# The pooled stage moved into the block of the later layers, with its products by feature rows and the first dense unit beside its last batch

## What is computed

```
x = layernorm(x + pooled(x));  x = layernorm(x + dense(x))
x = layernorm(x + heads(x));   x = layernorm(x + experts(x))

pooled: h  = layernorm(x) * g + b
        q, k, v = h Wq + bq, h Wk + bk, h Wv + bv
        w  = exp((q Wqa + bqa) / sqrt(512));  w = w / cumsum(w)
        mixed = cumsum(w * q) * k
        u  = exp((mixed Wka + bka) / sqrt(512));  u = u / cumsum(u)
        result = cumsum(u * mixed) * v
dense:  (silu(x Wg) * (x Wu)) Wd, weights dequantised from integers, 2048 inner features
```

## Time and profile before

| what | value |
|---|---|
| median of three runs | 3158.72 us |
| the profiled execution | 3159.45 us, its span 3157.6 us |
| busy in the span: PE, DVE, ACT, POOL | 2993.2, 1829.1, 1172.4, 1091.7 us |
| mean granted clock of TensorE | 0.973 |
| start of the dense products | 391.56 us |

### The profile page before, as it was taken

How to read it: one execution, slowest core, us unless ns; L and a number is a source line. 1 busy time by engine, 2 the same in 40 slices (tenths; PEclk the granted TensorE clock), 3 DMA queues, 4 the chain that set the end, 5 groups by cost and what they waited for, 6 DMA issues and landing times.

```text
span 3157.6 us, 38080 instructions
## 1 busy us (share of the span) xinstructions
PE 2993.2 (95%) x13984; PEld 2482.2 (79%) x13984; DVE 1829.1 (58%) x2654; ACT 1172.4 (37%) x2546; POOL 1091.7 (35%) x742
## 2 busy tenths in 40 slices
PE   6887399999999999999999999899999999999997
PEld 5676388888878888888888888677888888888886
DVE  4566433333368999999999999853222222222225
ACT  4343222222126666666666666521112111121110
POOL 3555223322223444444444444322223222232221
PEclk9888699999999999999999999999999999999998
DMA  3000110100013222232222222311000100001001
GB/s 121 1 1 1 46 40 21 40 21 21 7 62 81 59 68 63 62 83 61 64 67 61 64 77 70 92 41 40 21 21 21 40 21 21 21 21 41 1 1 54
DMA packets 61802, 135.39 MB, mean 43 GB/s; under 512 B 9136, under 2 KB 9520, under 8 KB 60464
## 3 DMA queue, kind: packets, MB, share of 16 engines
q1 hardware_dynamic: 61616, 132.95, 13.8%
HBM read 90.71 MB, written 8.65 MB: 31 GB/s over the span
## 4 chain that ended last, share of the span: by engine, by line
PE 83%; DVE 3%; issue 1%; SPq 0%; ACT 0%; POOL 0%; DMA 0%; POOLq 0%; DVEq 0%; ACTq 0%
PE A L44 6%; PE A L46 6%; PE B L44 6%; PE A L45 6%; PE B L46 6%; PE B L45 6%; PE S L44 5%; PE S L45 5%; PE S L46 5%; PE OP L44 5%; PE OP L46 5%; PE OP L45 5%; PE T L1202 2%; PE S L1186 2%; PE O L1196 2%; PE O L45 1%
## 5 line engine op out<-in xcount | busy, mean ns | idle before, releaser
L736 POOL TENSOR_TENSOR ffn_in_lo<-ffn_inner,ffn_in_hi 128x512 fp32r<-128x512 f32 x192 | 251.2, 1309 | 1112.8 <-ACT ffn_in_hi L732 1112.8
L732 ACT ACTIVATE ffn_in_hi<-ffn_inner 128x512 fp32r<-128x512 f32 x192 | 121.2, 632 | 562.3 <-DVE ffn_inner L748 362.2
L44 PE MATMUL S<-xT_hi,ffn_w_hi 128*128 128x512 f32 x768 | 298.8, 389 | 0.0
L45 PE MATMUL S<-xT_lo,ffn_w_hi 128*128 128x512 f32 x768 | 298.8, 389 | 0.0
L46 PE MATMUL S<-xT_hi,ffn_w_lo 128*128 128x512 f32 x768 | 298.8, 389 | 0.0
L748 DVE TENSOR_TENSOR ffn_inner<-S,ffn_gated 128x512 f32<-128x512 f32 x64 | 44.3, 692 | 291.4 <-PE S L46 284.9
L748 DVE TENSOR_TENSOR ffn_inner<-B,ffn_gated 128x512 f32<-128x512 f32 x64 | 44.3, 691 | 291.3 <-PE B L46 284.0
L1572 POOL TENSOR_TENSOR lag_rnorm<-lag_norm,minus_half 128x8 f32<-128x8 f32 x64 | 105.4, 1647 | 304.2 <-DVE lag_norm L1747 304.2
L44 PE MATMUL B<-xT_hi,lag_w_hi 128*128 128x512 f32 x512 | 206.8, 404 | 0.0
L44 PE MATMUL A<-xT_hi,lag_w_hi 128*128 128x512 f32 x512 | 205.9, 402 | 0.0
L46 PE MATMUL B<-xT_hi,lag_w_lo 128*128 128x512 f32 x512 | 200.6, 392 | 0.0
(11 more groups left out here) (295 smaller groups left out, 8024.0 us busy)
## 6 DMA issues: line engine op xcount, KB each, us to landing
lag_raw<-in_head_weights SPq DMA_DIRECT2D x64, 256.0 KB, 4.5
lag_b_row<-lag_b_scratch SPq DMA_DIRECT2D x64, 256.0 KB, 3.4
lag_rot_q<-lag_r SPq DMA_DIRECT2D x128, 128.0 KB, 2.3
lag_rot_k<-lag_r SPq DMA_DIRECT2D x128, 128.0 KB, 2.3
ffn_raw<-in_expert_gate SPq DMA_DIRECT2D x16, 512.0 KB, 3.6
ffn_raw<-in_expert_up SPq DMA_DIRECT2D x16, 512.0 KB, 4.5
ffn_raw<-in_expert_down SPq DMA_DIRECT2D x16, 512.0 KB, 5.2
x_tok<-in_x SPq DMA_DIRECT2D x4, 1024.0 KB, 5.4
```

The costliest lines, as they stand in the source:

```text
L44: pe.matmul(out, lh, rh, start=first and k == 0, stop=False)
L45: pe.matmul(out, lh, rl, start=False, stop=False)
L732: act.activation(self.in_hi[t % 2][:, f, :], self.inner[f], ACT.Copy).then_inc(self.s_hhi, 1)
L736: pool.tensor_tensor(self.in_lo[t % 2][:, f, :], self.inner[f], f32(self.in_hi[t % 2][:, f, :]), ALU.subtract).then_inc(self.s_hlo, 1)
```

## The change

The pooled stage becomes a class `Pooled` whose steps are small methods, and its instructions stand in the lists of `layers`, in one block. The identity's block goes, x of batch 0 is loaded in four parts, the dense weights' transfers wait for q(3) and for the mixed keys instead of a block. The banks are shared: `D` (T, O, OP0, OP1) for the projections, A and B for turning and for the inverses of ka, S0 and S1 for those of qa.

- **By feature rows.** q and v issue the first row of features for all four chunks, then the second, and so on; ka by pairs of chunks. q and ka wait for each low part where it is first used. v signals after each row, and ScalarE may write that row of h.
- **Transposes within.** Batch b+1 is turned after rows 1 and 2 of v(b); the turning back is split around q(b+1) in the middle slots.
- **Buffers.** The features replace the normalised rows in place (`xn`); the total goes to the output's own buffer, and an exponential waits only for the product with the gain.
- **Order of the other engines.** ScalarE takes two exponentials, then their inverses, then the other two. GpSimd mixes low parts and results. The second norm uses class `Norm`, and its normalising comes in ka's pooling.
- **Last batch.** Its qa pooling, ka and ka pooling alternate with the turning of batches 0 to 2 for the dense layer and with the first dense unit.

The heads' code changes in its semaphores only: some pairs are shared by two signals with doubled counts.

```
+    def products(self, pe, kind, b, rows, groups, ready, each=False, between=None):
+        hi, lo = rows
+        for n, ms in enumerate(groups):
+            for k in range(KC):
+                if n == 0:
+                    first = self.part(kind, b, 0) if kind in ("qa", "ka") else b * KC
+                    pe.wait_ge(ready, first + (k + 1 if each else KC))
+                for m in ms:
+                    at = self.place(kind, b, m)
+                    if k == 0:
+                        until(pe, self.s_ev, at - (KC - 1))
+                    cols = slice(m * P, (m + 1) * P)
+                    last = product(pe, self.banks[m], [(self.w_hi[kind][:, k, cols], self.w_lo[kind][:, k, cols])],
+                                   [(hi[:, k, :], lo[:, k, :])], first=k == 0, last=k == KC - 1)
...
+                if kind == "v" and k < KC - 1:
+                    last.then_inc(self.s_quarter, 1)
+                if between is not None:
+                    between(k)
...
+    def exponential(self, act, kind, b, m):
+        act.wait_ge(self.s_mm, self.place(kind, b, m) + 1)
+        if kind == "ka":
+            act.wait_ge(self.s_step["qa"], self.step(b, m, self.GAINED) + 1)
...
+        ROWS, PAIRS, CHUNKS = [range(KC)], [(0, 1), (2, 3)], [(m,) for m in range(KC)]
...
+                for b in range(BATCH - 1):
+                    pooled.products(pe, "v", b, h, ROWS, pooled.s_hlo, between=lambda k: pooled.turn(
+                        pe, b + 1, ((), (0, 1), (2, 3), ())[k]) if k in (1, 2) else None)
+                    if b:
+                        pooled.back(pe, b - 1, (0, 1), [A, B, A, B])
+                    pooled.products(pe, "q", b + 1, h, ROWS, pooled.s_hlo, each=True)
+                    if b:
+                        pooled.back(pe, b - 1, (2, 3), [A, B, A, B])
+                    pooled.products(pe, "ka", b, m, PAIRS, pooled.s_mlo, each=True)
+                    pooled.products(pe, "k", b + 1, h, CHUNKS, pooled.s_hlo)
+                    pooled.products(pe, "qa", b + 1, m, CHUNKS, pooled.s_mlo)
...
+                pooled.products(pe, "v", BATCH - 1, h, ROWS, pooled.s_hlo, between=early_turn)
+                pooled.back(pe, BATCH - 2, range(TPB), D)
+                pe.wait_ge(turn0.s_lo, TPB)
+                dense.gate_up(pe, 0, 0, (0,))
+                turn0.turn(pe, 1, D, norm0.s_row, lambda t: pe.wait_ge(pooled.s_add, (BATCH - 2) * TPB + t + 1))
+                pe.wait_ge(pooled.s_step["qa"], pooled.step(BATCH - 1, KC - 1, pooled.SECOND) + 1)
+                dense.gate_up(pe, 0, 0, (1,))
+                pe.wait_ge(turn0.s_lo, 2 * TPB)
+                pooled.products(pe, "ka", BATCH - 1, m, PAIRS, pooled.s_mlo, each=True)
+                dense.gate_up(pe, 0, 1, (0,))
+                turn0.turn(pe, 2, ENDS, norm0.s_row, lambda t: pe.wait_ge(
+                    pooled.s_ev, pooled.place("ka", BATCH - 1, t + 2) + 1), (0, 1))
+                dense.gate_up(pe, 0, 1, (1,))
+                turn0.turn(pe, 2, ENDS, norm0.s_row, lambda t: pe.wait_ge(turn0.s_lo, 2 * TPB + t - 1), (2, 3))
+                dense.down(pe, 0, 0, lambda tt: pe.wait_ge(*((turn0.s_lo, 2 * TPB + tt + 3) if tt < 2 else
+                                                             (dense.s_acc, tt - 1))), ENDS)
+                pe.wait_ge(turn0.s_lo, 3 * TPB)
+                dense.gate_up(pe, 0, 2, (0,))
+                pe.wait_ge(dense.s_acc, TPB)
+                pooled.back(pe, BATCH - 1, range(TPB), D)
...
+                def softmax(kind, b):
+                    for pair in PAIRS:
+                        for m in pair:
+                            pooled.exponential(act, kind, b, m)
+                        pooled.inverses(act, kind, b, pair)
...
+                    for pair in PAIRS:
+                        for m in pair:
+                            pooled.query_low(pool, b + 1, m)
+                        for m in pair:
+                            pooled.result(pool, "ka", b, m)
```

More of the change, by code:

```diff
@@ L1406, in _ @@
+                act.wait_ge(pooled.s_out["ka"], BATCH * KC)
+                dense.split_hi(act, 1)
+                turn0.high(act, 3)
+                step(dense, 0, 3)
+                for u in range(1, UNITS):
                     for t in range(BATCH):
@@ new lines, in _ @@
+                last = BATCH - 1
+                for m in range(KC):
+                    pooled.gain(pool, "qa", last, m)
+                dense.split_lo(pool, 0, (0, 1))
+                for m in range(KC):
+                    pooled.result(pool, "qa", last, m)
+                for m in range(KC):
+                    pooled.mixed_low(pool, last, m)
+                dense.split_lo(pool, 0, (2,))
+                norm0.root(pool, last - 1)
+                step(dense, 0, 0)
+                for m in range(KC):
+                    pooled.gain(pool, "ka", last, m)
@@ new lines, in _ @@
+                turn0.low(dve, 0, (2, 3))
+                pooled.gained(dve, "qa", last, (2, 3))
+                pooled.totals(dve, "qa", last, (2, 3))
+                for t in range(TPB):
+                    pooled.add_back(dve, last - 1, t, D)
+                pooled.second_statistics(dve, last - 1, range(TPB))
+                norm0.aggregate(dve, last - 1)
+                dense.chunk(dve, 0, 0, 0)
+                turn0.low(dve, 1)
+                norm0.normalise(dve, last - 1)
+                dense.chunk(dve, 0, 0, 1)
@@ new lines, in _ @@
+                pooled.sums(dve, "ka", last, (0, 1))
+                pooled.reciprocals(dve, "ka", last, (0, 1))
+                pooled.sums(dve, "ka", last, (2, 3))
+                pooled.gained(dve, "ka", last, (0, 1))
+                dense.chunk(dve, 0, 1, 0)
+                turn0.low(dve, 2, (0, 1))
+                pooled.totals(dve, "ka", last, (0, 1))
+                pooled.reciprocals(dve, "ka", last, (2, 3))
+                dense.chunk(dve, 0, 1, 1)
+                turn0.low(dve, 2, (2, 3))
@@ new lines, in _ @@
+                pooled.gained(dve, "ka", last, (2, 3))
+                pooled.totals(dve, "ka", last, (2, 3))
+                dense.add(dve, 0, 0, ENDS)
+                dense.dequantise(dve, 1)
+                dense.chunk(dve, 0, 2, 0)
+                for t in range(TPB):
+                    pooled.add_back(dve, last, t, D)
+                pooled.second_statistics(dve, last, range(TPB))
+                norm0.aggregate(dve, last)
+                dense.chunk(dve, 0, 2, 1)
+                norm0.normalise(dve, last)
@@ L1672, in _ @@
-                turn0.low(dve, 3)
-                chunks_of(dense, 0, 0)
-                for u in range(UNITS):
+                for u in range(1, UNITS):
                     for t in range(BATCH):
```

1038 lines of the change are left out of this document (521 added, 517 removed).

## The result

| | before | changed |
|---|---|---|
| median of 4 timed runs each | 3158.8 us (3158.1 to 3159.8) | 3106.05 us (3104.2 to 3107.2) |
| profiled execution (span) | 3159.45 (3157.6) | 3104.22 (3102.4) |
| mean granted clock | 0.973 | 0.988 |

The ratio is 0.9832, with a 95% interval of 0.9815 to 0.9849. The kernel is 1.7% faster. It was forecast to be 2.9% faster: the time is 37 us above the forecast of 3069 and outside the range of 3042 to 3094.

The account below looks back on a forecast made before the run. TensorE, busy 2993.2 of 3157.6 us, bounds the kernel; gains come where it waits or runs slowly. Start, slots and tail bring 393.6 us down to 255.7 + 32.6 + 15 = 303.3, 90.3 less: 3159.45 becomes 3069, range 3042 to 3094.

Parts of the forecast that it names:

- the last sentence of the sum: Merged counters, split xT tensors and stages from the second dense unit on cost nothing: same signal order, PE full there.
- Start: Up to the values of batch 0: they start at 49.7 instead of 57.70 us, 8.0 us earlier; bounds 2.2 and 11.
- the transfers: Loading x at once and in four quarters: 2.2 us earlier, and another 1.7 us for statistics run as quarters land.
- Slots: Three pooled-stage steps, values to next batch's values: 66, 70 and 70 us instead of 77.8, 74.9 and 75.0.
- the old waits: In the middle slots, PE's waits for the low parts of h and of the mixed keys go.
- the queries' low parts: Ahead of qa in each slot, PE waits 6.4 to 10 us, 8 taken, plus 2.9 for the clock behind it.
- Rival (a): Query low-part wait is only the undisturbed chain: slots 63, 65, 65, tail 9; 19 us less, 3050; chance 0.19.
- rival (b): Query wait is 12 us or more, slots stay at 75; only start and tail left: 3089; chance 0.18.
- the 65 us of such work: VectorE and GpSimd take turns on two-input SBUF operations, 37 plus 27.5 us a slot; no slot could be shorter.
- Tail: Last batch to dense layer: PE's 32.6 us of work plus 15 us of waits, where before took 106.1 plus 2.
- The six table loads: ScalarE's function-table loads between silus in the last batch, 1.28 us each; tail 15 us, 9 without (five x 1.3).
- Rival (e): Shared counters in the head stage hold PE at each of 64 steps; at 1.7 us each 109 us, 3178; chance 0.04.

Follow-up runs that it names:

- experiment 1: Changed kernel with the filler ahead of the late tiles at 120 words instead of 128, so they begin 32 bytes lower: 3061.8 us, ratio 0.9685.
- experiment 3: Kernel before with only xT_hi and xT_lo split into eight tensors of one group each: 3159.6 us, ratio 0.9999.
- experiment 11: Kernel of experiment 1 with projections q and ka by output chunks again, each waiting for all four low parts: 3089.3 us, ratio 0.9780.
- experiment 8: Kernel of experiment 1 with the queries' high parts ahead of ka's last two inverses and their low parts ahead of gains 2 and 3: 3049.1 us.
- experiment 12: Kernel of experiment 8 with GpSimd's gains and low parts two by two, qa awaiting low parts singly, one table request before the last softmax: 3046.4 us.

## Why the prediction failed

**The step that failed** is the last sentence of the sum, by which "the stages from the second dense unit on cost nothing". The merged counters and the split of xT, which stand in the same sentence, do cost nothing (experiments 1 and 3). What cost 44 us was where the change puts tensors. The reason that I gave, "each engine signals in the old order, and PE is full there", was about waits; I took a TensorE that is always busy for one that runs as fast as before. The diff had the edit (`scale_down` moved, `norm0` added, a filler of 168 words cut by 40), and I read it as bookkeeping. In size: 4464 matmuls of the units behind group 3 at 0.0067 us more are 30 us. By the traces of the changed kernel and the first experiment the rest of the dense layer takes 490.8 and 480.9 us, the experts 1103.3 and 1083.9, 29 us together, and the stage of the heads between them 1165.5 and 1153.6, 12 us on 3168 matmuls with xT (by their distances from start to start, 0.0042 us more each, it would be 13). Together 41, the difference of the two traces from group 3 on (2759.5 and 2718.4). The values and the first three groups add 2.2 by their count (336 matmuls). The other 3.4 of the 44.5 us are no more than what executions differ by: in the eight kernels without the fault this stretch takes 2711 to 2718 us, in the kernel before 2715.

The Trainium skill ("SBUF — State Buffer", Who interferes with whom) gives TensorE two read ports, for the moving operand and for weight loads, which are independent. Weight loads lie beside matmuls in every trace here, but the pace of 0.2267 or 0.2333 us depends on where the two operands lie to each other. That fits two reads that are not wholly independent, but that it is these reads that meet is my reading, which no run shows apart.

**The other steps**, with the fault taken out (3061.8 against 3069):
- Start: 8.0 us forecast; 9.15 in the trace of the changed kernel (57.70 against 48.55), but 7.0 to 7.5 in the seven traces whose first projection begins at the lower clock, as it does before (0.76 us in the earlier trace rows). So the forecast, which had that clock in its 13.0 us, was 0.5 to 1 us too high. By the runs the feature rows carry 3.6 (the values start at 53.90 in experiment 11, 50.33 in 1) and the transfers 0.7 to 2.4, where I had 3.9; the rest was not tried apart.
- Slots: 66, 70, 70 forecast; 63.9, 68.2, 68.2, of which 0.3 each is the fault in the values (48 matmuls). The mechanism was right: the old waits went and the queries' low parts came, with 5.0, 7.4 and 7.4 us, low in my 6.4 to 10. Rival (a), 63, 65, 65, was below, rival (b) above. The chunk behind the wait took 5.0 us instead of 2.7, 2.3 more, where I had 2.9. VectorE and GpSimd do take turns, as the earlier trace rows showed: two low parts took 3.88 and 2.93 us beside VectorE's products and scans instead of 2.5. But the 65 us of such work in a slot, which the prediction held against shorter slots, are no floor: with the same operations the slots of batches 1 and 2 take 61.9 to 63.1 us in experiments 8 and 12. Its sum counts 3.8 us of normalisings, which have one large input.
- Tail: 108.1 - 47.6 = 60.5 us of gain forecast. Measured by the gate of group 3, 99.7 less the 36.6 that the values of batch 3 start earlier: 63.1. The six table loads and the waits came where the forecast had them. The one at the down product was 5.25 us, as forecast, those at the turning and at the add 0.7 and 0.95, where I had 3 and 2 to 3. The share of the loads was 3.2 us in waits, where I had 6.
- Rival (e), the counters of the heads, is refuted by experiment 1: with them in place the heads run as before (mean distance of its matmuls with xT from 1000 to 1900 us 0.2287 us, before 0.2284).
- Rival (b) was added up loosely: slots of 77.8, 74.9 and 75.0 us give back 21.8 us, not 14 + 6, which makes 3091. It changes nothing here.

So without the fault all terms together were 7 us too careful, inside the forecast's own range of 3057 to 3079, with the slots and the tail too long and the start slightly too good.

## What to carry to other kernels

When a change adds, drops or resizes any on-chip tensor, compare the start addresses of the moving and the stationary operand of each matmul before and after (modulo 256 bytes fits the runs here), and count what the allocator really takes for small tiles. "The engine is full there" says nothing about its pace: compare the distance of two matmul starts, or the mean of one group, in stages that the change does not touch. And work that is moved ahead on a shared engine only moves the wait unless what it passes has slack; read the next chain before counting the gain.

## What the runs showed of the hardware

- A 128x512 matmul of this type starts every 0.2267 us when the regions of its two operands differ by 0 or 256 bytes in their start addresses (the tiles within them lie at multiples of 512), and every 0.2333 us (0.0067 us, 2.9%, more) at differences of 32, 64 and 128. This holds for the products with xT; of the values' products at 64 bytes one kind in three ran at full pace. An equal shift of both costs next to nothing: in the changed kernel q, k and the down products have both operands 32 bytes off and run at 389 and 390 ns. Only the first five matmuls of a down product are late, 0.023 us together, and only where slow products stand ahead of them.
- In the heads the same fault costs less, 0.0042 us a matmul with xT (0.2329 and 0.2287 us, changed kernel and first experiment, 1000 to 1900 us); the distance there is above 0.2267 even without it.
- A change between silu, exponential and logarithm costs one load of 1.28 us each time, and the next operation starts 1.29 us behind the load's start. The Trainium skill ("ScalarE: Activation LUTs", What ACT_TABLE_LOAD costs) adds a drain to 2.66 us; no row here shows one. Asking once for the table with both functions took four of the six loads away.
